# A fused graph network layer on one core: gcn_b moved into the value tiles, one ScalarE pass and a VectorE low half over the mixed blocks

## The chip, the core and the metric

The kernel runs on one core of one Trainium2 chip. The metric is the device time of a launch in microseconds (us), taken as the median of the runs. Below, PE is TensorE, DVE is VectorE, ACT is ScalarE, POOL is GpSimd and SP is SyncE, which here issues the loads and stores.

## The reference

x holds 128 graphs of 64 nodes with 384 features, adj their 0/1 adjacency. gcn_b is a bias of 384 numbers, drawn non-zero here. With an adjacency of only 0 and 1 each edge has the same kind, and the kernel uses that. A path for other adjacencies is branched over on the chip and does not run.

```python
adj = dep_type_matrix != 0
hi_t = einsum('bid,de->bie', h, W1_w[:HID])[:, :, None, :] + (edge term) + W1_b
hj_t = einsum('bjd,de->bje', h, W2_w[:HID])[:, None, :, :] + (edge term) + W2_b
relevance = sum(hi_t * hj_t, axis=-1)
A = softmax(where(adj, relevance, -1e9), axis=2)
h_syn = relu(einsum('bij,bjd->bid', A, h) @ gcn_w + gcn_b)
return layernorm(h + h_syn @ Wo_w + Wo_b)
```

The rows of A sum to one. So a row vector added to every row of h @ gcn_w comes out of A @ (h @ gcn_w) unchanged.

## The kernel before

The 8192 tokens are cut into 16 groups (0 to 15, LAST is 15) of 512 tokens: four "pairs" q of 128 tokens, each two graphs. The three chunks of 128 features are c, d or f in the code (C is 3). For accuracy the large products are done in three passes: an operand is split into a high half (rounded to fp32r) and a low half (the rest), and PE adds high x high, high x low and low x high. These are the three lines L415 to L417 of the helper `three`, and L506, L507 and L512 for the output product.

Each engine runs its own program, written out by hand, group by group in `body(g, par)`, and the engines meet at semaphores only. Groups 2 to 13 run in a loop of two bodies, groups 0, 1, 14 and 15 are written out. In body g the engines do this:

- PE: `mix(g-1)` (L492, the attention weights times the value tiles of the group before), `score_stage(g)` (L437), `value(g+1, q)` for the four pairs (x @ gcn_w into PSUM banks 1 to 4), `out(g-1)` (times Wo), `turn(g)` (L472, transposes the weights), `proj(g+1)`. Body 15 has no value and no projection. Its order is mix(14), score(15), `out` of group 13 pairs 2 and 3, `out` of group 14 pairs 0 and 1, turn(15), `out` of 14 pair 2, mix(15), `out` of 14 pair 3, and then `out_last(15)`.
- ACT: `hidden(g-1)` reads the mixed blocks from PSUM, one block for each chunk f. Blocks 0 and 1 lie in banks 6 and 7, block 2 in banks 4 and 5. For each block it makes two passes of Relu with the bias gcn_b: one writes hs_sb in full precision (L775), one writes the rounded high half hs_hi (L777; in group 14 its home is xt_hi). Then come the exponentials (`weigh`), a rounding of x, `row_terms`, and copies out of PSUM.
- DVE: the masked scores (L914, L918, L920), `value_out` (L819, a copy of the value tile out of PSUM), `low_half(g-1)` (L905, hs_sb minus hs_hi, both in SBUF), the softmax weights (L932, L934), the sum with x (`add_x`, L827), its statistics (L832) and the normalisation (L849).
- POOL: x plus Wo_b (L1098), the low half of x (L1089), the inverse deviation (L1109).

PE waits in three places for what the change touches. `value(g+1, 3)` writes bank 4, where mixed block 2 lies, and waits on `hshi`. `out(g-1)` waits on `hslo` (all low halves). `out` of group 14, pairs 1 and 2, reuses banks in which the output of group 13 lay, and waits until `add_x` of group 13, pair 2 and pair 3, has read them.

At the end, `hidden(15)` on ACT is followed by `normalise_last` for group 13 (L726). That result is stored, and DVE's first `add_x` of group 15 waits for this store (semaphore `stored`), since it writes the same buffer y_sb. After it DVE works through the four pairs of group 15, and POOL, DVE and SP finish each.

## Time and profile before

| what | value |
|---|---|
| median of 3 runs | 389.34 us (389.31 to 390.85) |
| the profiled execution, its own time | 389.31 us |
| its span in the trace | 387.5 us |
| PE busy | 373.5 us (96%) |
| DVE busy | 215.4 us (56%) |
| ACT busy | 170.8 us (44%) |
| POOL busy | 150.4 us (39%) |
| share of PE in the chain that ended last | 90% |

The span is what the trace holds, from the first instruction to the last. The execution's own time is 1.8 us longer. A busy share is an average. A span of 387.5 us with PE busy for 373.5 us leaves 14 us in which PE does nothing, and the question is where in the program they lie.

### The profile page before, as it was taken

To read this page: it belongs to the slowest core of one execution; us is meant where nothing else is said; L and a number is where in the kernel's file an instruction comes from. 1 tells how busy PE (TensorE), PEld (TensorE's weight loads), DVE (VectorE), ACT (ScalarE), POOL (GpSimd) and SP (SyncE) were. 2 spreads that over 40 slices of the span, in tenths; PEclk is the share of its full clock that TensorE was granted. 3 is DMA by queue.
4 is the path that set the end of the run, shared out by engine and by line. 5 is a ranking of instruction groups with operands and counts; after the bars stand their busy time and mean duration, and the time that the engine had idled before them with its cause. 6 is when DMAs were issued, how large, how long until landed. Compare 5 with 4: busy or idle time off the path is not lost.

```text
span 387.5 us, 10043 instructions
## 1 busy us (share of the span) xinstructions
PE 373.5 (96%) x3977; PEld 342.2 (88%) x3977; DVE 215.4 (56%) x528; ACT 170.8 (44%) x389; POOL 150.4 (39%) x133
## 2 busy tenths in 40 slices
PE   8899999999999999999999999999999999999990
PEld 4789898999989899998989899898989989898890
DVE  1635175674637467563646656363765636374954
ACT  1635552616354271625427162633616263444372
POOL 0123454270815326081633608062350807243123
PEclk9999999999999999999999999999999999999997
DMA  7922023508052350706244170614317071531023
GB/s 222 319 99 81 18 82 80 181 10 249 1 181 78 88 169 16 242 0 185 73 106 151 19 238 0 196 61 135 122 24 233 0 216 41 152 109 42 2 83 125
DMA packets 34820, 42.89 MB, mean 111 GB/s; under 512 B 10096, under 2 KB 29040, under 8 KB 34800
## 3 DMA queue, kind: packets, MB, share of 16 engines
q1 hardware_dynamic: 34144, 41.92, 35.9%
q10 hardware_dynamic: 656, 0.70, 0.6%
q8 instruction: 13, 0.21, 0.2%
q14 instruction: 7, 0.06, 0.1%
HBM read 30.03 MB, written 12.58 MB: 110 GB/s over the span
## 4 chain that ended last, share of the span: by engine, by line
PE 90%; DMA 3%; ACT 2%; DVE 2%; POOL 1%; SPq 1%; issue 0%; DVEq 0%
PE banks L415 18%; PE banks L417 17%; PE banks L416 17%; PE banks L506 8%; PE banks L507 8%; PE banks L512 8%; PE banks L492 6%; PE banks L437 6%; DMA gcn_sb<-in_gcn_w_dram 2%; ACT hs_sb L775 1%; PE banks L472 1%; DMA out_dram<-y_sb 1%; POOL rstd L1109 1%; DVE xt_lo L905 0%; ACT xt_hi L777 0%; ACT hs_hi L777 0%
## 5 line engine op out<-in xcount | busy, mean ns | idle before, releaser
L1098 POOL TENSOR_TENSOR x_sb<-x_sb,wob_sb 128x1536 f32<-128x1536 f32 x15 | 52.5, 3503 | 178.0 <-DVE weights L934 178.0
L415 PE MATMUL banks<-gcn_hi,xt_hi 128*128 128x386 f32 x192 | 66.7, 347 | 1.1 <-DVE gcn_lo L877 1.1
L417 PE MATMUL banks<-gcn_hi,xt_lo 128*128 128x386 f32 x192 | 65.0, 339 | 0.0
L416 PE MATMUL banks<-gcn_lo,xt_hi 128*128 128x386 f32 x192 | 65.0, 339 | 0.0
L914 DVE SCALAR_TENSOR_TENSOR rel<-banks,srow,adj_sb 128x64 f32<-128x64 f32 x64 | 13.8, 278 | 86.2 <-PE banks L437 84.8
L506 PE MATMUL banks<-wo_hi,hs_hi 128*128 128x384 f32 x180 | 61.0, 339 | 0.0
L507 PE MATMUL banks<-wo_lo,hs_hi 128*128 128x384 f32 x180 | 61.0, 339 | 0.0
L512 PE MATMUL banks<-wo_hi,hs_lo 128*128 128x384 f32 x180 | 60.6, 339 | 0.0
L701 ACT ACTIVATE gt_sb<-banks,r_sb 128x512 f32<-128x512 f32 x45 | 30.9, 687 | 65.9 <-PE banks L417 65.9
L415 PE MATMUL banks<-xt_hi,m_hi 128*128 128x512 f32 x144 | 57.6, 400 | 0.4 <-DVE hg_sb L819 0.4
L417 PE MATMUL banks<-xt_hi,m_lo 128*128 128x512 f32 x144 | 56.7, 394 | 0.0
L416 PE MATMUL banks<-xt_lo,m_hi 128*128 128x512 f32 x144 | 56.4, 392 | 0.0
L1089 POOL TENSOR_TENSOR xt_lo<-xt_sb,xt_hi 128x1536 fp32r<-128x1536 f32 x15 | 52.6, 3505 | 3.3 <-ACT xt_hi L695 3.3
L827 DVE TENSOR_TENSOR y_sb<-banks,x_sb 128x384 f32<-128x384 f32 x60 | 33.4, 557 | 30.4 <-PE banks L512 30.3
L819 DVE COPY hg_sb<-banks 128x385 f32<-128x385 f32 x64 | 35.6, 556 | 22.2 <-PE banks L417 22.1
L775 ACT ACTIVATE hs_sb<-banks,bias_sb 128x512 f32<-128x512 f32 x48 | 33.4, 695 | 16.3 <-PE banks L492 16.3
L415 PEld LDWEIGHTS banks<-gcn_hi,xt_hi 128*128 128x128 f32 x192 | 36.2, 188 | 2.3 <-issue 1.2
L832 DVE BATCH_NORM_STATS2 stats<-y_sb 128x6 f32<-128x384 f32 x64 | 35.9, 561 | 2.2
L416 PEld LDWEIGHTS banks<-gcn_lo,xt_hi 128*128 128x128 f32 x192 | 36.5, 190 | 0.0
L417 PEld LDWEIGHTS banks<-gcn_hi,xt_lo 128*128 128x128 f32 x192 | 36.3, 189 | 0.0
L789 ACT COPY at_sb<-banks 128x256 f32<-128x256 f32 x16 | 6.0, 374 | 68.0 <-PE banks L472 68.0
L506 PEld LDWEIGHTS banks<-wo_hi,hs_hi 128*128 128x128 f32 x180 | 33.8, 188 | 0.1
(87 smaller groups left out, 580.8 us busy)
## 6 DMA issues: line engine op xcount, KB each, us to landing
xt_sb<-in_x_t_dram SPq DMA_DIRECT2D x15, 768.0 KB, 4.6
x_sb<-in_x_dram SPq DMA_DIRECT2D x15, 768.0 KB, 5.6
out_dram<-y_sb SPq DMA_DIRECT2D x30, 384.0 KB, 5.8
adj_sb<-in_adj_dram SPq DMA_DIRECT2D x32, 64.0 KB, 2.3
xt_sb<-in_x_t_dram SPq DMA_DIRECT2D x2, 384.0 KB, 8.5
xt_sb<-in_x_dram SPq DMA_DIRECT2D x1, 768.0 KB, 6.2
out_dram<-y_sb SPq DMA_DIRECT2D x4, 192.0 KB, 1.9
w1t_sb<-in_w_t_dram ACTq DMA_DIRECT2D x3, 192.0 KB, 6.3
```

Source lines behind the costliest of these rows:

```text
L415: pe.matmul(acc, a_hi, b_hi, start=first, stop=False)
L416: pe.matmul(acc, a_hi, b_lo, start=False, stop=False)
L417: return pe.matmul(acc, a_lo, b_hi, start=False, stop=last)
L506: pe.matmul(acc, hs_home(g)[0][:, c, ts], wo_hi[:, c, :], start=(c == 0), stop=False)
L507: pe.matmul(acc, hs_home(g)[0][:, c, ts], wo_lo[:, c, :], start=False, stop=False)
L512: mm = pe.matmul(out_bank(g, q)[:, 0:HID], hs_home(g)[1][:, c, ts], wo_hi[:, c, :], start=False, stop=(c == C - 1))
L775: act.activation(by_graph(hs_sb[:, f, :]), mixed(f), ACT.Relu, bias=gb_sb[:, f:f + 1]).then_inc(hsr, 1)
L819: dve.tensor_copy(hg_sb[:, slot, q, :], VALUE_BANK[q][:, 0:HID + 1]).then_inc(hg_ready, 1)
L827: dve.tensor_tensor(y_sb[:, slot, q, :], out_bank(g, q)[:, 0:HID], x_home(g, slot)[:, q, :], ALU.add).then_inc(added, 1)
L832: dve.bn_stats(stats[:, q, :], y_sb[:, slot, q, :]).then_inc(statd, 1)
L1089: pool.tensor_tensor(xt_lo[:, slot], xt_sb[:, slot], f32(xt_hi[:, slot]), ALU.subtract).then_inc(xlo, 1)
L1098: pool.tensor_tensor(x_home(g, slot), x_home(g, slot), wob_sb[:].rearrange("p (o n) -> p o n", o=1).to_broadcast([P, PAIRS, HID]), ALU.add ...
```

## The change

gcn_b is no longer ACT's bias. At the start DVE puts it on a diagonal (three tensor_scalar of the identity with gb_sb), PE spreads it over all rows with a matmul of ones into bank 4, and DVE copies it to the tile gb_row. `value_out` becomes a tensor_tensor that adds gb_row to the value tile while it leaves PSUM. ACT then makes one pass for each block, without bias, straight to the high half. The low half is made by DVE from PSUM itself, max(mixed, 0) minus hs_hi, in two instructions for each block, one for each bank. The blocks are taken in the order 0, 2, 1, on ACT, on DVE and in the output product. ACT's pass over block 1 waits until DVE has read block 0, which lies in the same banks. `low_half(g-1)` moves to the head of DVE's body, ahead of the masked scores. PE's wait ahead of `value(g+1, 3)` is on `hslo` now.

```diff
         attn = sb("attn", [P, C, P])
         weights = sb("weights", [P, PAIRS, NODES])
         at_sb = sb("at_sb", [P, MIX])
-        hs_sb = sb("hs_sb", [P, C, GT])
+        gb_diag = sb("gb_diag", [P, HID])
+        gb_row = sb("gb_row", [P, HID + 1])
+        hs_sb = sb("hs_sb", [P, C, P])
         hs_hi = sb("hs_hi", [P, C, GT], F32R)
         hs_lo = sb("hs_lo", [P, C, GT], F32R)
...
+        GB_BANK = bank[4]
+        BLOCKS = 0, 2, 1
...
                 elif q == 3 and not static(g, 1):
-                    pe.wait_ge(hshi, C * (g - 1))
+                    pe.wait_ge(hslo, C * (g - 1))
...
                 acc = out_bank(g, q)[:, 0:HID]
-                pe.matmul(acc, hs_home(g)[0][:, c, ts], wo_hi[:, c, :], start=(c == 0), stop=False)
+                pe.matmul(acc, hs_home(g)[0][:, c, ts], wo_hi[:, c, :], start=(c == BLOCKS[0]), stop=False)
                 pe.matmul(acc, hs_home(g)[0][:, c, ts], wo_lo[:, c, :], start=False, stop=False)
             def out_low(g, q, c):
                 ts = slice(q * P, (q + 1) * P)
                 mm = pe.matmul(out_bank(g, q)[:, 0:HID], hs_home(g)[1][:, c, ts], wo_hi[:, c, :],
-                               start=False, stop=(c == C - 1))
-                if c == C - 1:
+                               start=False, stop=(c == BLOCKS[-1]))
+                if c == BLOCKS[-1]:
                     mm.then_inc(out_mm, 1)
...
+            pe.wait_ge(ones_ready, 1)
+            pe.wait_ge(gb_diag_ready, 1)
+            pe.matmul(GB_BANK[:, 0:HID], ones[:].to_broadcast([P, P]), gb_diag[:],
+                      start=True, stop=True).then_inc(gb_mm, 1)
...
             def out_last(g):
-                for c in range(C):
-                    pe.wait_ge(hshi, C * g + c + 1)
+                for n, c in enumerate(BLOCKS):
+                    pe.wait_ge(hshi, C * g + n + 1)
                     for q in range(2):
-                        if c == 0:
+                        if n == 0:
                             pe.wait_ge(added, PAIRS * (g - 1) + q + 2)
                         out_high(g, q, c)
-                    pe.wait_ge(hslo, C * g + c + 1)
+                    pe.wait_ge(hslo, C * g + n + 1)
                     for q in range(2):
                         out_low(g, q, c)
...
             def hidden(g):
                 act.wait_ge(mix_mm, g + 1)
-                for f in range(C):
-                    act.activation(by_graph(hs_sb[:, f, :]), mixed(f), ACT.Relu,
-                                   bias=gb_sb[:, f:f + 1]).then_inc(hsr, 1)
-                    act.activation(by_graph(hs_home(g)[0][:, f, :]), mixed(f), ACT.Relu,
-                                   bias=gb_sb[:, f:f + 1]).then_inc(hshi, 1)
+                for n, f in enumerate(BLOCKS):
+                    if n == C - 1:
+                        act.wait_ge(hslo, C * g + 1)
+                    act.activation(by_graph(hs_home(g)[0][:, f, :]), mixed(f), ACT.Relu).then_inc(hshi, 1)
...
             def value_out(g, slot, q):
                 dve.wait_ge(value_mm, PAIRS * g + q + 1)
-                dve.tensor_copy(hg_sb[:, slot, q, :], VALUE_BANK[q][:, 0:HID + 1]).then_inc(hg_ready, 1)
+                if static(g, 0) and q == 0:
+                    dve.wait_ge(gb_row_ready, 1)
+                dve.tensor_tensor(hg_sb[:, slot, q, :], VALUE_BANK[q][:, 0:HID + 1], gb_row[:],
+                                  ALU.add).then_inc(hg_ready, 1)
...
             dve.tensor_tensor(c1_sb[:], C_BANK[0][:, 0:C], b1_sb, ALU.add).then_inc(c1_ready, 1)
+            dve.memset(gb_row[:, HID:HID + 1], 0.0)
+            dve.wait_ge(ident_ready, 1)
+            for c in range(C):
+                a = dve.tensor_scalar(gb_diag[:, c * P:(c + 1) * P], ident[:], gb_sb[:, c:c + 1], None, ALU.mult)
+            a.then_inc(gb_diag_ready, 1)
...
+            dve.wait_ge(gb_mm, 1)
+            dve.tensor_copy(gb_row[:, 0:HID], GB_BANK[:, 0:HID]).then_inc(gb_row_ready, 1)
...
-            def low_half(g, chunks):
-
-                for f in chunks:
-                    dve.wait_ge(hsr, C * g + f + 1)
-                    dve.wait_ge(hshi, C * g + f + 1)
-                    dve.tensor_tensor(hs_home(g)[1][:, f, :], hs_sb[:, f, :], f32(hs_home(g)[0][:, f, :]),
-                                      ALU.subtract).then_inc(hslo, 1)
+            def low_half(g, parts):
+
+                for n in parts:
+                    f = BLOCKS[n]
+                    dve.wait_ge(hshi, C * g + n + 1)
+                    for h in range(HALVES):
+                        a = dve.scalar_tensor_tensor(by_graph(hs_home(g)[1][:, f, :])[:, h], mixed(f)[:, h], 0.0,
+                                                     by_graph(f32(hs_home(g)[0][:, f, :]))[:, h], ALU.max,
+                                                     ALU.subtract)
+                    a.then_inc(hslo, 1)
             def body(g, par):
+                if not static(g, 0):
+                    low_half(g - 1, range(C))
                 dve.wait_ge(score_mm, g + 1)
...
                 if static(g, LAST):
                     add_x(g - 2, par, 2)
-                    low_half(g - 1, range(C))
                 elif static(g, 0):
                     value_out(1, 1, 0)
                     value_out(1, 1, 1)
                 else:
                     value_out(g + 1, 1 - par, 0)
-                    low_half(g - 1, range(C))
                     value_out(g + 1, 1 - par, 1)
```

DVE in body 15, before. The rows begin with the masked scores of group 15 (rel), and xt_lo is the home of group 14's low half:

```order
L914 SCALAR_TENSOR_TENSOR rel<-banks,srow,adj_sb 128x64 x4
L918 TENSOR_TENSOR rel<-rel,neg_sb 128x256
L920 TENSOR_REDUCE nmax<-rel 128x4
L827 TENSOR_TENSOR y_sb<-banks,x_sb 128x384
L905 TENSOR_TENSOR xt_lo<-hs_sb,xt_hi 128x512 x3
L932 RECIPROCAL rsum<-psum_row 128x4
L934 TENSOR_TENSOR weights<-prob,rsum 128x256
L832 BN_STATS stats<-y_sb 128x6
L827 TENSOR_TENSOR y_sb<-banks,x_sb 128x384
```

The same place after, from the head of the body:

```order
L925 SCALAR_TENSOR_TENSOR xt_lo<-banks,xt_hi 128x4x64 x6
L938 SCALAR_TENSOR_TENSOR rel<-banks,srow,adj_sb 128x64 x4
L942 TENSOR_TENSOR rel<-rel,neg_sb 128x256
L944 TENSOR_REDUCE nmax<-rel 128x4
L839 TENSOR_TENSOR y_sb<-banks,x_sb 128x384
L954 RECIPROCAL rsum<-psum_row 128x4
L956 TENSOR_TENSOR weights<-prob,rsum 128x256
L844 BN_STATS stats<-y_sb 128x6
L839 TENSOR_TENSOR y_sb<-banks,x_sb 128x384
```

The low half went from behind the first add of group 13 (pair 2) to ahead of the scores, and has six instructions for three.

ACT in body 15, before, with what each waits for: hidden of group 14, the exponentials, the copy of the turned weights, and the first rows of hidden of group 15:

```order
L775 ACTIVATE hs_sb<-banks,bias_sb 128x2x4x64 [waits mix_mm]
L777 ACTIVATE xt_hi<-banks,bias_sb 128x2x4x64
L775 ACTIVATE hs_sb<-banks,bias_sb 128x2x4x64
L777 ACTIVATE xt_hi<-banks,bias_sb 128x2x4x64
L775 ACTIVATE hs_sb<-banks,bias_sb 128x2x4x64
L777 ACTIVATE xt_hi<-banks,bias_sb 128x2x4x64
L767 ACTIVATE prob,psum_row<-rel,nmax 128x64 [waits masked]
L767 ACTIVATE prob,psum_row<-rel,nmax 128x64 x3
L789 COPY at_sb<-banks 128x256 [waits turn_mm]
```

The same place after, up to the normalisation of group 13 (L746):

```order
L787 ACTIVATE xt_hi<-banks 128x2x4x64 [waits mix_mm]
L787 ACTIVATE xt_hi<-banks 128x2x4x64
L787 ACTIVATE xt_hi<-banks 128x2x4x64 [waits hslo]
L777 ACTIVATE prob,psum_row<-rel,nmax 128x64 [waits masked]
L777 ACTIVATE prob,psum_row<-rel,nmax 128x64 x3
L798 COPY at_sb<-banks 128x256 [waits turn_mm]
L787 ACTIVATE hs_hi<-banks 128x2x4x64 [waits mix_mm]
L787 ACTIVATE hs_hi<-banks 128x2x4x64
L787 ACTIVATE hs_hi<-banks 128x2x4x64 [waits hslo]
L746 ACTIVATE y_sb<-y_sb,nmr,rstd 128x384 [waits nmr_ready]
```

Six passes became three, and the third waits for DVE.

DVE at the start of the program, after. The rows run from the vectors c1 and c2 to the first two value tiles:

```order
L875 MEMSET gb_row 128x1
L878 TENSOR_SCALAR gb_diag<-ident,bias_sb 128x128 x3
L882 TENSOR_TENSOR c_sb<-c_sb 128x3
L886 TENSOR_TENSOR xt_lo<-xt_sb,xt_hi 128x3x256
L890 TENSOR_TENSOR gcn_lo<-gcn_sb,gcn_hi 128x384 x3
L894 TENSOR_TENSOR gcn_lo<-banks,gcn_hi 128x2 x3
L897 COPY gb_row<-banks 128x384
L899 TENSOR_TENSOR xt_lo<-xt_sb,xt_hi 128x3x256
L903 TENSOR_TENSOR m_lo<-banks,m_hi 128x384 x3
L830 TENSOR_TENSOR hg_sb<-banks,gb_row 128x385 x2
```

The first two of these rows and the copy to gb_row are new, and everything else stands in the order of before (the last row was two copies). On PE the matmul that spreads gcn_b stands ahead of the small products of line L547 (`r_stage`).

## Rows read from the trace of the kernel before

**Rows 1.** Busy time by engine in a stretch: length, PE, PEld, DVE, ACT, POOL, clock
```profile
200.00:225.00 25.00, 25.00 (x336) 22.91 (x338) 12.90 (x32) 10.73 (x25) 9.34 (x7) 1.00 0.41 120
```

**Rows 2.** Timeline of group 8: start, duration, engine, line, operation
```profile
182.13 0.86 DVE L914 SCALAR_TENSOR_TENSOR rel<-banks,srow,adj_sb 128x64 f32<-128x64 f32 x4 [5.55 <-PE banks L437]
...
186.89 0.34 PE L415 MATMUL banks<-gcn_hi,xt_hi 128*128 128x386 f32 x1
...
194.83 0.38 PE L472 MATMUL banks<-ident,weights 128*128 128x128 f32 x2
```

**Rows 3.** Timeline of the start of the program
```profile
7.08 6.06 PE L539 MATMUL banks<-w2t_sb,w1t_sb 128*128 128x385 f32 x18 [0.44 <-DVE c_sb L861]
...
14.84 0.42 PE L415 MATMUL banks<-gcn_hi,xt_hi 128*128 128x386 f32 x1 [1.14 <-DVE gcn_lo L877]
...
15.74 1.48 DVE L884 TENSOR_TENSOR m_lo<-banks,m_hi 128x384 fp32r<-128x384 f32 x3
...
19.59 0.48 PE L415 MATMUL banks<-xt_hi,m_hi 128*128 128x512 f32 x1
```

**Rows 4.** Groups by line and shape: count, busy us, mean ns of one
```profile
L819 DVE COPY hg_sb<-banks 128x385 f32<-128x385 f32 x64 | 35.6, 556 | 22.2 <-PE banks L417 22.1
L827 DVE TENSOR_TENSOR y_sb<-banks,x_sb 128x384 f32<-128x384 f32 x60 | 33.4, 557 | 30.4 <-PE banks L512 30.3
...
L777 ACT ACTIVATE hs_hi<-banks,bias_sb 128x512 fp32r<-128x512 f32 x45 | 31.4, 698 | 0.0
...
L905 DVE TENSOR_TENSOR hs_lo<-hs_sb,hs_hi 128x512 fp32r<-128x512 f32 x45 | 28.5, 684 | 1.0 <-ACT hs_hi L777 1.0
...
L695 ACT CAST xt_hi<-xt_sb 128x1536 fp32r<-128x1536 f32 x15 | 22.2, 1482 | 20.8 <-DMA xt_sb<-in_x_t_dram 20.8
...
L914 DVE SCALAR_TENSOR_TENSOR rel<-banks,srow,adj_sb 128x64 f32<-128x64 f32 x64 | 13.8, 278 | 86.2 <-PE banks L437 84.8 <-ACT srow L717 1.4
...
L918 DVE TENSOR_TENSOR rel<-rel,neg_sb 128x256 f32<-128x256 f32 x16 | 6.8, 425 | 0.5
...
L789 ACT COPY at_sb<-banks 128x256 f32<-128x256 f32 x16 | 6.0, 374 | 68.0 <-PE banks L472 68.0
```

**Rows 5.** The same view, VectorE alone: 384 columns, from SBUF and from PSUM
```profile
L873 DVE TENSOR_TENSOR gcn_lo<-gcn_sb,gcn_hi 128x384 fp32r<-128x384 f32 x3 | 1.5, 554 | 0.7 <-ACT gcn_hi L735 0.7
L884 DVE TENSOR_TENSOR m_lo<-banks,m_hi 128x384 fp32r<-128x384 f32 x3 | 1.5, 550 | 0.0
```

**Rows 6.** Timeline of body 15, up to the turn and what follows it
```profile
356.84 0.69 ACT L775 ACTIVATE hs_sb<-banks,bias_sb 128x512 f32<-128x512 f32 x1 [0.90 <-PE banks L492]
...
358.37 0.86 DVE L914 SCALAR_TENSOR_TENSOR rel<-banks,srow,adj_sb 128x64 f32<-128x64 f32 x4 [4.25 <-PE banks L437]
...
361.22 1.29 DVE L905 TENSOR_TENSOR xt_lo<-hs_sb,xt_hi 128x512 fp32r<-128x512 f32 x2
...
361.51 0.22 ACT L767 ACTIVATION_READ_ACCUMULATOR prob<-rel,nmax 128x1 f32 x1
362.42 0.17 DVE L932 RECIPROCAL rsum<-psum_row 128x4 f32<-128x4 f32 x1
362.56 0.44 PE L506 MATMUL banks<-wo_hi,xt_hi 128*128 128x384 f32 x1 [0.86 <-DVE xt_lo L905]
...
363.44 0.54 DVE L827 TENSOR_TENSOR y_sb<-banks,x_sb 128x384 f32<-128x384 f32 x1
```

**Rows 7.** Timeline of the tail
```profile
365.93 0.42 PE L506 MATMUL banks<-wo_hi,xt_hi 128*128 128x384 f32 x1
...
369.31 0.42 DVE L949 TENSOR_REDUCE row_max<-adj_max 128x1 f32<-128x256 int32 x1
369.39 0.69 ACT L775 ACTIVATE hs_sb<-banks,bias_sb 128x512 f32<-128x512 f32 x1 [2.80 <-PE banks L492]
...
372.82 2.52 ACT L726 ACTIVATE y_sb<-y_sb,nmr,rstd 128x384 f32<-128x384 f32 x4
...
376.75 0.56 DVE L827 TENSOR_TENSOR y_sb<-banks,xt_sb 128x384 f32<-128x384 f32 x1 [2.83 <-DMA out_dram<-y_sb]
```

More of the change, by code:

```diff
@@ L198, in gnn_layernorm_kernel @@
         c_mm = sem("c_mm")
+        gb_diag_ready = sem("gb_diag_ready")
+        gb_mm = sem("gb_mm")
+        gb_row_ready = sem("gb_row_ready")
         c12_sb_ready = sem("c12_sb_ready")
@@ L230, in gnn_layernorm_kernel @@
         mix_mm = sem("mix_mm")
-        hsr = sem("hsr")
         hshi = sem("hshi")
@@ L306, in hs_home, with mixed, by_graph @@
             return (xt_hi[:, 0], xt_lo[:, 0]) if static(g, LAST - 1) else (hs_hi, hs_lo)
+        def mixed(f):
+            at, b0, b1 = MIX * (f % 2), MIX_BANK[0][f], MIX_BANK[1][f]
+            halves = banks[:, b0:b1 + 1, at:at + MIX]
+            return halves.rearrange("p h (q n) -> p h q n", n=NODES)
+        def by_graph(row):
+            return row.rearrange("p (q h n) -> p h q n", h=2, n=NODES)
         def run(eng, body):
@@ L576, in out @@
                         pe.wait_ge(hg_ready, PAIRS * (g + 2) + 1)
-                    for c in range(C):
+                    for c in BLOCKS:
                         out_high(g, q, c)
@@ L581, in out_last @@
             def out_last(g):
-                for c in range(C):
-                    pe.wait_ge(hshi, C * g + c + 1)
+                for n, c in enumerate(BLOCKS):
+                    pe.wait_ge(hshi, C * g + n + 1)
                     for q in range(2):
-                        if c == 0:
+                        if n == 0:
                             pe.wait_ge(added, PAIRS * (g - 1) + q + 2)
                         out_high(g, q, c)
-                    pe.wait_ge(hslo, C * g + c + 1)
+                    pe.wait_ge(hslo, C * g + n + 1)
                     for q in range(2):
@@ L593, in out_last @@
                 for q in range(2, PAIRS):
-                    for c in range(C):
+                    for c in BLOCKS:
                         out_high(g, q, c)
@@ L751, in _ @@
             row_terms(0, 0)
-            def mixed(f):
-                at, b0, b1 = MIX * (f % 2), MIX_BANK[0][f], MIX_BANK[1][f]
-                halves = banks[:, b0:b1 + 1, at:at + MIX]
-                return halves.rearrange("p h (q n) -> p h q n", n=NODES)
-            def by_graph(row):
-                return row.rearrange("p (q h n) -> p h q n", h=2, n=NODES)
             def weigh(g):
```

## The prediction

> **What bounds the kernel now.** I read the busy times by stretch first. Between 50 and 350 us PE is busy for all 25.00 of every 25 us, at a granted clock of 1.00; one of the twelve stretches is shown, with DVE busy for 12.90 and ACT for 10.73 [rows 1]. So there the time is PE's own work, and taking a pass from ACT buys nothing by itself: the change can gain only at the two ends, and can lose in the middle if it makes PE wait. Second, the timeline of one middle group shows how much room there is. The scores' first DVE instruction starts at 182.13, PE starts value pair 3 at 186.89, and transposes the softmax weights at 194.83 [rows 2]. Third, the start: PE is idle for 1.14 us ahead of its first value tile [rows 3]. Fourth, body 15 and the tail: PE is idle for 0.86 us because DVE's low half of group 14 comes late [rows 6]. And DVE's first add of group 15 waits for a store of group 13, which ACT could normalise only after its six hidden passes [rows 7].
>
> **Prices.** Value tiles: a copy of 385 columns out of PSUM takes 556 ns, an add of a PSUM and an SBUF operand over 384 columns 557 ns [rows 4]. So copy to add costs 0.
>
> ACT's pass: with a bias it takes 698 ns for 512 columns. Without a bias there are 374 ns for 256 columns and 1482 ns for 1536, which makes 0.87 ns a column and 0.60 us for 512 [rows 4]. I take 0.60 us, and a next pass 0.51 us after it. The other end is 0.70 us.
>
> Low half: no row shows this instruction. The nearest are a two-operand DVE instruction with 256 columns, 425 ns, and with 512, 684 ns [rows 4]. Two of 512 follow each other 0.60 us apart (1.29 for two) [rows 6], so 256 columns should follow 0.36 us apart. I take 0.42 us for one and 0.36 + 0.42 = 0.78 us for a block, against 0.68 before. The same form of instruction with 64 columns takes 278 ns [rows 4], where 256 and 512 columns lead to 0.23. The excess of 0.05 may be fixed (it reads a scalar and an integer operand which the low half doesn't), or a second cycle for each column. The second is the upper end: 0.69 us for one, 0.60 apart, 1.29 for a block. The lower end is 0.78 less 0.1, one block at today's price.
>
> The source moves from SBUF to PSUM. The rows have 384 columns from SBUF at 554 ns and from PSUM at 550 [rows 5], no difference. The Trainium skill (VectorE: DVE Perf Modes, section on the TRN2 errata) gives VectorE's fixed part as 58 cycles from SBUF and 120 from PSUM, which would speak against this change: 62 cycles at the page's 0.96 GHz are an estimated 0.065 us for each of the six instructions of a group. By the page the gain below would be about 0.5 us smaller, some 388.4 us. The trace does not agree with it at 384 columns, and I go by the trace.
>
> Hand-over from one engine to another: DVE's low halves end at 361.22 + 1.29 = 362.51, PE starts at 362.56 [rows 6]. I take 0.1 us as an estimate for ACT to DVE and back, where more is to be done than a matmul's start.
>
> **The start.** Added on DVE: a memset and three tensor_scalar of 128 columns while it has nothing due but c12. Added on PE: one fp32 matmul of 384 columns. Nine such (18 passes) take 6.06 us, 0.67 us each. PE has 1.14 us idle just behind it [rows 3], so it ends inside that wait: 0. If it cost more than 1.14 us, what is over would move everything; I keep 0.3 us for that. Added on DVE ahead of the second low half of x: a copy of 384 columns, 0.55 us by its like [rows 4]. It pushes m_lo from 15.74 + 1.48 = 17.22 to about 17.8, and PE wants it at 19.59 [rows 3]. Cost 0, with 1.8 us left.
>
> **The middle, 13 times the same.** Put the mix's end so that ACT starts hidden at 0. In body 15 ACT starts at 356.84 and the scores 1.53 us later, at 358.37 [rows 6]; the middle is alike. After the change, in body 15's clock:
> - ACT block 0: 356.84 to 357.44; block 2 from 357.35 to 357.95.
> - DVE low half 0: 357.54 to 358.32. ACT block 1 waits for it: 358.42 to 359.02.
> - DVE low half 2 until 359.04, low half 1 from 359.12 to 359.90.
> - The scores start at 359.84 in place of 358.37: 1.47 us later.
>
> In the middle's clock the low halves end at 182.13 + 1.53 = 183.66, 3.2 us before value pair 3, which now needs them [rows 2]. Before the change they were ready later than that, and the output product still never waited. The scores' delay passes to the softmax weights. Before, the reciprocal came 4.05 us after the scores in body 15 [rows 6]. Even 4.05 + 1.47 puts it at 187.7, and the turn is at 194.83 [rows 2]. Queued behind the scores on DVE are value tiles 0 and 1, whose banks nobody needs before the end of the output product. POOL starts after the weights, some tenths later, and has over 10 us. SP's adjacency load waits for the scores, but stands ahead of a wait for the output's adds, which is later. So the middle costs and gains 0. ACT's three passes saved, 45 in the middle and more, are free time on an engine that already waits.
>
> **Body 15.** The low half is no longer behind the scores, so PE need not wait for it: it ends at 359.90, and PE comes to it 1.13 us before 362.56, at 361.43. (The idle time is 0.86. PE's matmuls overlap by 0.17 us, and the first after a wait lasts 0.44 for 0.34 [rows 2, 6].) What is late next is the add of group 13, pair 3. Its chain is scores, maximum, exponentials, reciprocal, weights, statistics, add. The exponentials ended at 361.51 + 0.22 = 361.73; they end at 363.20 now, and the reciprocal starts at 363.30 in place of 362.42, 0.88 us later. (Before, it waited for the low halves, now for ACT.) The add goes from 363.44 to 364.32, ends at 364.86, and PE may start output pair 2 of group 14 at 364.96. Its own pace would bring it there at 365.93 - 1.13 = 364.80 [rows 6, 7]. It waits 0.16, so 0.97 us of the 1.13 is kept when mix(15) starts.
>
> **The tail.** hidden(15) on ACT may start at 369.39 - 0.97 = 368.42. But DVE, 0.88 us late since the reciprocal, has caught up only partly. Of that lateness 0.1 goes at its second add of group 14 and 0.38 at its third, where DVE waited before, so row_max starts at 369.71 for 369.31. Low half 0 follows at 370.07 and ends at 370.85, ACT's block 1 starts at 370.95, and group 13's normalisation 0.51 later, at 371.46, in place of 372.82 [rows 7]: 1.36 us sooner. From there to DVE's first add of group 15 it is 376.75 - 372.82 = 3.93 us of ACT and DMA work that doesn't change. DVE's four pairs follow back to back. PE's last output pairs end before DVE needs them, since PE is some tenths ahead as well. So the end moves by 1.36 us.
>
> **Sum.** The profiled execution took 389.31 us, the median is 389.34, and the span is 387.5 (387.5 + 1.8 around it). 389.31 - 1.36 = 387.95; I say 388.0 us. The likeliest case's own range is 387.4 to 388.6.
>
> **Rivals.**
> 1. DVE's low half is slow and the end comes later than before. Mechanism: the ring ACT block 0, DVE low half 0, ACT block 1, low half 1 stands ahead of the scores, and twice in body 15 PE and ACT wait for DVE. With the upper end of 1.29 us a block: the scores start at 361.15 (2.78 late), the reciprocal at 364.61, the add of pair 3 ends at 366.17, and PE is 0.3 us later than before instead of 0.97 earlier. Row_max starts at 371.0, low half 0 ends at 372.7, and the normalisation starts at 373.3, 0.45 late: 389.8 us. It decides from about 0.63 us for one instruction. For it speaks the 278 ns at 64 columns; against it, that two other operands can explain them, and the 557 ns of the PSUM add.
> 2. The gain is taken elsewhere: the store lands when it did or PE's waits in body 15 grow, and the tail keeps only a part. With ACT's pass at 0.70 the same walk gives a gain of 1.1 us; with the store's time of 3.93 stretched by a few tenths, or 0.3 us at the start, 0.5. That is 388.8 us. For it: the chain has five hand-overs that I only estimate.
> 3. More is gained: everything behind the low halves goes at ACT's pace, not DVE's. Then the normalisation starts at 368.42 + 3 x 0.51 = 369.95 and the tail becomes PE's: PE ends 0.97 earlier and DVE's last pair follows it, some 2.0 us in all, 387.3. Against it: row_max on DVE stands in front.
> 4. The middle waits after all: each group would have to lose 0.13 us or more to be seen. It would take low halves 3.2 us later than I put them; 13 x 0.15 = 2 us gives 391.3. Nothing in the rows speaks for it.
>
> **How the numbers follow.** No change can be told within 0.5% of 389.34, from 387.4 to 391.3. Forecast 0.62, rival 1 0.14, rival 2 0.15, rival 3 0.06, rival 4 0.03. The range for 8 in 10 runs from 387.2 to 389.7, the forecast's own range with rival 2 and most of rival 1. Faster by over 0.5% holds rival 3 and the forecast's edge, 0.07; slower holds rival 4 and a little of rival 1, 0.04; no change 0.89.
>
> **What would show it.** Low-half instructions of 128x256 near 0.42 us, ACT's pass near 0.60, the value tile's add near 0.56. Middle stretches still 25.00 busy. The 0.86 us in front of group 14's output gone, and a wait of 0.1 to 0.3 us one product later, for y_sb. Row_max some 0.4 later, the normalisation 1.2 to 1.5 earlier, and the wait for the store smaller. It would be wrong if PE showed a wait in every group, if a low-half instruction took over 0.6 us, or if the matmul for gcn_b moved the first value tile past 14.84.

## The result, and the profile after

| | before | after |
|---|---|---|
| median, on one chip side by side (15 runs each) | 390.51 us | 387.05 us (384.89 to 388.71) |
| ratio of after to before | | 0.990 (0.988 to 0.993) |
| the profiled execution, its own time | 389.31 us | 387.49 us |
| its span | 387.5 us | 385.5 us |
| PE, DVE, ACT busy | 373.5, 215.4, 170.8 us | 373.8, 220.4, 142.6 us |

By the ratio, which goes by the means, the change gains 3.8 us (2.7 to 4.8); the medians are 3.5 apart. The forecast was 1.36. The time lies below the forecast range, if barely.

I cut both spans at the copies of the turned weights (`at_sb`, one for each group), since these follow a fixed place in PE's program. The third column is a kernel that is explained below: the changed one, with hs_hi, hs_lo and what follows them put back to the addresses of before.

| stretch, us | before | after | after, tiles as before |
|---|---|---|---|
| start to the first at_sb copy | 39.17 | 40.48 | 40.21 |
| 14 groups, up to the copy of group 14 | 309.88 | 308.26 | 309.89 |
| to the copy of group 15 (body 15) | 17.16 | 16.00 | 16.03 |
| to the start of DVE's last write of y_sb | 16.60 | 15.56 | 15.54 |
| to the end of the span (the last store) | 4.69 | 5.20 | 4.83 |

Two stretches hold the gain: the groups of the middle, 1.62 us, which I had put at nothing, and body 15 with the tail, 1.16 + 1.04 = 2.20 us, where I had put 1.36. Together they make 3.82 us, as much as the means differ. The start was later by 1.31 us in this one execution, and the last stretch, which ends with a store, longer by 0.5; so these two spans are only 2.0 us apart.

The stretch of the middle after, which answers to [rows 1] (same columns). PE is still busy all the time:

```profile
200.00:225.00 25.00, 25.00 (x314) 22.82 (x315) 13.22 (x35) 9.45 (x22) 9.39 (x7) 1.00 0.43 119
```

So this view can't show the gain: a PE that is never idle can still do a group in less time. The copies of the turned weights show it. First three in a row of before, then three of after (start, duration):

```profile
195.24 0.37 ACT L789 COPY at_sb<-banks 128x256 f32<-128x256 f32 x1 [4.76 <-PE banks L472]
217.67 0.37 ACT L789 COPY at_sb<-banks 128x256 f32<-128x256 f32 x1 [4.76 <-PE banks L472]
240.10 0.37 ACT L789 COPY at_sb<-banks 128x256 f32<-128x256 f32 x1 [4.76 <-PE banks L472]
```

```profile
195.72 0.37 ACT L798 COPY at_sb<-banks 128x256 f32<-128x256 f32 x1 [4.64 <-PE banks L488]
218.02 0.37 ACT L798 COPY at_sb<-banks 128x256 f32<-128x256 f32 x1 [4.65 <-PE banks L488]
240.33 0.37 ACT L798 COPY at_sb<-banks 128x256 f32<-128x256 f32 x1 [4.65 <-PE banks L488]
```

A group took 22.43 us and takes 22.31. Of the groups by line and shape, the output matmuls alone got shorter. Lines of before (a value matmul first), then of after:

```profile
L416 PE MATMUL banks<-gcn_lo,xt_hi 128*128 128x386 f32 x192 | 65.0, 339 | 0.0
L506 PE MATMUL banks<-wo_hi,hs_hi 128*128 128x384 f32 x180 | 61.0, 339 | 0.0
```

```profile
L432 PE MATMUL banks<-gcn_lo,xt_hi 128*128 128x386 f32 x192 | 65.0, 338 | 0.0
...
L522 PE MATMUL banks<-wo_hi,hs_hi 128*128 128x384 f32 x180 | 60.5, 336 | 0.0
...
L528 PE MATMUL banks<-wo_hi,hs_lo 128*128 128x384 f32 x180 | 59.9, 336 | 0.0
```

From the first output matmul of a group to what follows the last it takes 6.24 us in place of 6.35, which is 0.1733 us for each of the 36 in place of 0.1764. These 0.114 us are nearly all of the 0.12; another 0.005 came off the value matmuls. The mean times of the value and projection matmuls stayed within 1 ns.

What answers to [rows 4], with the waits behind the bar:

```profile
L925 DVE SCALAR_TENSOR_TENSOR hs_lo<-banks,hs_hi 128x256 fp32r<-128x256 f32 x90 | 32.7, 418 | 68.0 <-ACT hs_hi L787 67.9
L787 ACT ACTIVATE hs_hi<-banks 128x512 fp32r<-128x512 f32 x45 | 25.3, 596 | 20.9 <-PE banks L508 15.4 <-DVE hs_lo L925 5.5
L830 DVE TENSOR_TENSOR hg_sb<-banks,gb_row 128x385 f32<-128x385 f32 x64 | 34.7, 555 | 23.6 <-PE banks L433 23.6
```

The three prices of the forecast stand: 0.42 us for a low half of 256 columns, 0.60 for ACT's pass, 0.56 for the value tile's add. ACT waits for DVE inside the ring, 5.5 us in all, and PE for neither.

Body 15 after, which answers to [rows 6]:

```profile
356.53 1.08 ACT L787 ACTIVATE xt_hi<-banks 128x512 fp32r<-128x512 f32 x2 [0.90 <-PE banks L508]
357.16 2.18 DVE L925 SCALAR_TENSOR_TENSOR xt_lo<-banks,xt_hi 128x256 fp32r<-128x256 f32 x6 [3.34 <-ACT xt_hi L787]
...
357.95 0.60 ACT L787 ACTIVATE xt_hi<-banks 128x512 fp32r<-128x512 f32 x1 [0.34 <-DVE xt_lo L925]
...
359.25 0.85 DVE L938 SCALAR_TENSOR_TENSOR rel<-banks,srow,adj_sb 128x64 f32<-128x64 f32 x4
...
361.18 0.35 PE L522 MATMUL banks<-wo_hi,xt_hi 128*128 128x384 f32 x1
...
362.52 0.18 DVE L954 RECIPROCAL rsum<-psum_row 128x4 f32<-128x4 f32 x1 [1.04 <-ACT prob L777]
...
364.46 0.42 PE L522 MATMUL banks<-wo_hi,xt_hi 128*128 128x384 f32 x1
```

And the tail, which answers to [rows 7]:

```profile
368.73 0.42 DVE L971 TENSOR_REDUCE row_max<-adj_max 128x1 f32<-128x256 int32 x1
...
369.06 0.74 DVE L925 SCALAR_TENSOR_TENSOR hs_lo<-banks,hs_hi 128x256 fp32r<-128x256 f32 x2
...
369.84 0.60 ACT L787 ACTIVATE hs_hi<-banks 128x512 fp32r<-128x512 f32 x1 [0.83 <-DVE hs_lo L925]
...
370.34 2.49 ACT L746 ACTIVATE y_sb<-y_sb,nmr,rstd 128x384 f32<-128x384 f32 x4
...
374.23 0.56 DVE L839 TENSOR_TENSOR y_sb<-banks,xt_sb 128x384 f32<-128x384 f32 x1 [2.02 <-DMA out_dram<-y_sb]
...
380.30 0.48 DVE L861 TENSOR_SCALAR y_sb<-y_sb,mv,rstd 128x384 f32<-128x384 f32 x1 [0.60 <-POOL rstd L1131]
```

In all these rows the clock stands 0.31 us earlier than before (the mix of group 14 starts at 354.83 for 355.14), so 0.31 is to be added to a time of after when it is held against one of before. PE's wait of 0.86 us for the low half is gone. DVE's first add of group 15 still waits for the store, for 2.02 us where it was 2.83.

### The profile page after: what moved, and what is told of

Its sections match the earlier page's. It is cut to its first block, busy times and chain, and to the rows that moved or that the text cites. A ratio compares the mean times of both kernels' runs of the same rounds, so it can differ in the third digit from the quotient of the medians.

```text
span 385.5 us, 10018 instructions
## 1 busy us (share of the span) xinstructions
PE 373.8 (97%) x3979; PEld 342.0 (89%) x3979; DVE 220.4 (57%) x581; ACT 142.6 (37%) x341; POOL 150.7 (39%) x133
## 4 chain that ended last, share of the span: by engine, by line
PE 92%; DVE 4%; POOL 1%; ACT 1%; DMA 1%; issue 1%; DVEq 0%
PE banks L431 18%; PE banks L433 17%; PE banks L432 17%; PE banks L523 7%; PE banks L528 7%; PE banks L522 7%; PE banks L508 6%; PE banks L453 6%; PE banks L555 2%; PE banks L536 1%; DVE stats L844 1%; PE banks L488 1%; DMA out_dram<-y_sb 1%; DVE y_sb L839 1%; POOL rstd L1131 1%
## 5 line engine op out<-in xcount | busy, mean ns | idle before, releaser
L925 DVE SCALAR_TENSOR_TENSOR hs_lo<-banks,hs_hi 128x256 fp32r<-128x256 f32 x90 | 32.7, 418 | 68.0 <-ACT hs_hi L787 67.9
L830 DVE TENSOR_TENSOR hg_sb<-banks,gb_row 128x385 f32<-128x385 f32 x64 | 34.7, 555 | 23.6 <-PE banks L433 23.6
L777 ACT ACTIVATE prob<-rel,nmax 128x64 f32<-128x64 f32 x64 | 21.5, 337 | 39.5 <-DVE nmax L944 39.5
L523 PEld LDWEIGHTS banks<-wo_lo,hs_hi 128*128 128x128 f32 x180 | 33.8, 188 | 0.0
```

What stands on the lines that cost most here:

```text
L523: pe.matmul(acc, hs_home(g)[0][:, c, ts], wo_lo[:, c, :], start=False, stop=False)
L830: dve.tensor_tensor(hg_sb[:, slot, q, :], VALUE_BANK[q][:, 0:HID + 1], gb_row[:], ALU.add).then_inc(hg_ready, 1)
L925: a = dve.scalar_tensor_tensor(by_graph(hs_home(g)[1][:, f, :])[:, h], mixed(f)[:, h], 0.0, by_graph(f32(hs_home(g)[0][:, f, :]))[:, h], A ...
```

## The experiments

The theories. T1: the middle's 1.6 us come from where hs_hi and hs_lo lie in SBUF, the on-chip memory that all tiles share. They are the stationary tiles of the output product, those that PE loads ahead of each matmul. hs_sb shrank from 6144 to 1536 bytes a partition and gb_diag and gb_row came in, so hs_hi starts at 148800 in place of 150304. Rival: three ACT passes fewer, or other accesses, speed PE up. T2: the tail goes by group 13's normalisation on ACT, its store, and the add that waits for it. T3: the start is hidden. In an edit, pad_a and pad_b are unused columns of four bytes.

**e1, before with hs_hi moved by 32 bytes.**

```diff
+        pad_a = sb("pad_a", [P, 8])
         hs_hi = sb("hs_hi", [P, C, GT], F32R)
         hs_lo = sb("hs_lo", [P, C, GT], F32R)
+        pad_b = sb("pad_b", [P, 8])
         y_sb = sb("y_sb", [P, 2, PAIRS, HID])
```

> The kernel before with 32 bytes of padding ahead of hs_hi and 32 behind hs_lo: these two tiles begin at a multiple of 64 bytes, all others stay within a 64-byte line where they were. Placement theory: output matmuls that read hs_hi and hs_lo start every 0.1735 us instead of 0.177, a group takes 22.31 us instead of 22.43, and the time falls by 1.6 to 1.9 us (ratio 0.995 to 0.996). Rival (the faster groups come from fewer ScalarE passes and less SBUF traffic): nothing changes, ratio 1.000.

Measured: 388.00 us, ratio 0.994 (0.991 to 0.998); a group takes 22.31 us and the output matmul 336 ns; body 15 stays at 17.16. 32 unused bytes bring the whole gain of the middle, and no engine's program is changed.

**e2, after with hs_hi moved by 32 bytes**, the same edit.

> The changed kernel with the same 32 bytes of padding: hs_hi and hs_lo begin 32 bytes past a multiple of 64, as they did before the change. Placement theory: a group takes 22.43 us again, and 1.6 to 1.9 us of the gain are lost (ratio to before about 0.994 to 0.995). Rival (fewer passes): groups stay at 22.31 us, ratio 0.990.

Measured: 385.74 us, 0.990 (0.986 to 0.993); 22.33 us a group. So "32 past a multiple of 64 is slow" fell.

**e5, after with hs_lo and what follows moved, not hs_hi** (pad_a behind hs_hi).

> The changed kernel with padding between hs_hi and hs_lo only: hs_hi begins at a multiple of 64 bytes, hs_lo 32 past one. If the place of the stationary tile itself counts, only the output matmul that reads hs_lo (one in three) is slower, and a group takes 22.35 us, between 22.31 and 22.43. If it is a matter of hs_hi alone, 22.31.

Measured: 386.7 us in a single run, 22.30 us a group. hs_lo's place within 64 bytes doesn't matter to the group here. But the single passes shifted against each other: the output matmuls have means of 335, 334 and (with hs_lo) 338 ns for 336, 336 and 336, and the projection's of 404, 388 and 393 for 399, 392 and 394, though no tile of the projection had moved. e2, where hs_lo lies at the same address, has the projection at 403, 389 and 392. So the mean of one pass is weak evidence for a place; the group's period is what I go by.

**e6, after with the rows of gcn_hi and gcn_lo lengthened to 1600 bytes.**

```diff
-        gcn_hi = sb("gcn_hi", [P, C, HW], F32R)
+        gcn_hi = sb("gcn_hi", [P, C, HID + 16], F32R)[:, :, 0:HW]
```

> The changed kernel with the rows of gcn_hi and gcn_lo, the streamed operand of the value matmuls, padded from 1544 to 1600 bytes, so that each of their six rows begins at a multiple of 64. If the place of a streamed operand counts too, the value matmuls go from 0.176 to 0.174 us, a group gets 0.05 to 0.1 us shorter and the time 0.8 to 1.5 us. If only the stationary tile's place counts: no change against the changed kernel, ratio to before 0.990.

Measured: 386.71 us, 0.992 (0.989 to 0.995); 22.39 us a group, slower by 0.08. What changed is the projection. Its streamed tiles xt_hi and xt_lo were moved by the edit, by 320 bytes, and m_hi and m_lo stayed. Its 27 matmuls of a group take 6.45 us for 6.37, with means of 404, 395 and 394 ns for 399, 392 and 394. So places have a price in other products too. The 404 ns alone would not show it, since e5 has them as well, at no cost to the group. The value matmuls gained nothing by the longer rows (6.46 us a group for 6.45).

**e9, e10, e11: other pads**, 96 bytes (after), 96 bytes (before), 160 bytes (after).

> The kernel after with 96 bytes (per partition) put ahead of hs_hi: it starts at 148896, which is 32 bytes past a multiple of 128, as in the kernel before (150304); hs_lo and y_sb move by 96 and 128. Theory A, the output product is slower when its stationary tile starts 32 past a multiple of 128: a group of the middle takes 22.43 us as before, and the output matmul has a mean of 339 ns. Rival B, the position within 128 bytes doesn't matter: 22.31 to 22.33 us and 336 ns.

> The kernel before with 96 bytes put ahead of hs_hi: it starts at 150400, a multiple of 128, where the pad of 32 bytes had put it 64 past one. Theory A: 22.31 us for a group of the middle. Rival B, the slow place of the kernel before is one single address and any move away from it helps: 22.31 us too, so this run can't tell A from B; it can only make both fall, with 22.43 us. Theory C, the group's time goes by something else that the pad of 32 bytes changed by chance: anything from 22.31 to 22.43.

> The kernel after with 160 bytes put ahead of hs_hi: it starts at 148960, 96 bytes past a multiple of 128, the class that the pad of 32 bytes gave (22.33 us). Theory A: 22.33 us again. Rival B: 22.31 to 22.33. With 22.39 or more the period goes by whole addresses, not by their place within 128 bytes.

Measured: 22.33, 22.32 and 22.31 us a group (385.8, 387.8 and 385.6 us, single runs). Theory A, 32 past a multiple of 128, fell with e9.

**e13, after with every tile from hs_hi on at its address of before** (pad_a of 376 columns, 1504 bytes).

> The kernel after with 1504 unused bytes per partition ahead of hs_hi. Then hs_hi (150304), hs_lo (156448), y_sb (162592) and every tile behind them start exactly where they do in the kernel before; the program is otherwise the kernel after. Theory P, the place of the tiles alone gave the middle's 1.6 us: 22.42 or 22.43 us for a group of the middle, a mean of 339 ns for the output matmul, and a time about 1.6 us above that of the kernel after, ratio some 0.995. Rival Q, the gain in the middle comes from the change itself (three ACT passes less, or reads of PSUM in place of SBUF) and the pads of the earlier runs did something else: 22.31 us, ratio 0.990.

Measured: 388.54 us, 0.993 (0.989 to 0.998). Its output matmul, and its line for the low half's product:

```profile
L523 PE MATMUL banks<-wo_hi,hs_hi 128*128 128x384 f32 x180 | 61.0, 339 | 0.0
...
L529 PE MATMUL banks<-wo_hi,hs_lo 128*128 128x384 f32 x180 | 60.5, 339 | 0.0
```

The copies of the turned weights come 22.43 us apart again:

```profile
196.29 0.37 ACT L799 COPY at_sb<-banks 128x256 f32<-128x256 f32 x1 [4.76 <-PE banks L489]
218.72 0.37 ACT L799 COPY at_sb<-banks 128x256 f32<-128x256 f32 x1 [4.76 <-PE banks L489]
```

With ACT's passes, VectorE's reads of PSUM and every other instruction as in the kernel after, the addresses alone bring the 1.6 us back. The rival Q fell by this period; the ratio's interval would hold both 0.995 and 0.990. Body 15 and the stretch behind it keep the times of after (16.03 and 15.54 us), so their gain is the change's own.

**e14, before with y_sb alone moved; e15, before with all three moved by 128 bytes; e16, after with all three moved by 96.**

> The kernel before with 32 bytes put ahead of y_sb alone: hs_hi and hs_lo stay at 150304 and 156448, y_sb and what follows it move from 162592 to 162624. Theory P1, the place of the output product's own operand sets its pace: 22.43 us for a group, 339 ns. Rival P2, the tile that the other engines write meanwhile (y_sb) does: 22.31 us, 336 ns.

> The kernel before with 128 bytes ahead of hs_hi: hs_hi 150432, hs_lo 156576, y_sb 162720, all three still 32 bytes past a multiple of 128. Theory P3, it is the place within 128 bytes of all three together (the earlier pads broke it for one of them each time): 22.43 us. Rival P4, whole addresses decide: any other value, 22.31 the likeliest.

> The kernel after with 96 bytes ahead of hs_hi and none ahead of y_sb: hs_hi 148896, hs_lo 155040, y_sb 161184, all three 32 bytes past a multiple of 128 as in the kernel before, but 1408 bytes lower. Theory P3: 22.43 us. Rival P4: 22.31 to 22.33.

Measured: 22.43, 22.33 and 22.33 us a group. e14 shows that moving y_sb and what follows takes no part, so it is the place of the product's own operands, hs_hi and hs_lo. Neither of the two was moved alone from the slow place, so which of them counts is open. e15 and e16 let P3 fall. All places of hs_hi together:

| hs_hi at | kernels | us a group | output matmul, ns |
|---|---|---|---|
| 150304 | before, e3, e13, e14 | 22.43 | 339 |
| 150336, 150400, 150432 | e1, e10, e15 | 22.31, 22.32, 22.33 | 334 to 337 |
| 148800 | after, e4, e5, e7, e8, e12, e17, e18 | 22.30 to 22.31 | 334 to 338 |
| 148832, 148896, 148960 | e2, e9 and e16, e11 | 22.33, 22.33, 22.31 | 336 to 337 |
| 149120 | e6 | 22.39 (projection) | 336 |

One place of nine is slow, and no rule on the place within 64 or 128 bytes that I tried picks it out. That the place decides is shown; what is special about it stays open.

**e3 and e4, an earlier normalisation**, in before and in after: group 13's pairs 2 and 3 are normalised ahead of `hidden(15)`.

```diff
+                    normalise_last(LAST - 2, 1, 1, (2, 3))
                     hidden(g)
...
             run(act, body)
-            normalise_last(LAST - 2, 1, 1, (2, 3))
```

> The kernel before, with ScalarE's last normalisation of group 13 put ahead of the hidden passes of group 15, where ScalarE sits idle for 2.8 us. Tail theory (the end is set by hidden passes, then this normalisation, then its store, then the first add of group 15): the wait of 2.8 us for the store goes, the first add starts when PE has its product (about 374.4 instead of 376.75 in the trace), 2.2 to 2.4 us gained, ratio 0.994. Rival (the tail is set by the output product on PE): 0 to 0.3 us.

> The changed kernel with the same move. Tail theory: the first add of group 15 starts at about 372.7 instead of 374.2, 1.5 us gained on the changed kernel, ratio to before about 0.986. Rival: nothing, 0.990.

Measured: 387.97 us, 0.993 (0.990 to 0.997), and 385.03 us, 0.986 (0.981 to 0.991). The first add of group 15 in e3, then in e4:

```profile
373.50 0.56 DVE L827 TENSOR_TENSOR y_sb<-banks,xt_sb 128x384 f32<-128x384 f32 x1 [0.47 <-PE banks L512]
```

```profile
371.27 0.56 DVE L839 TENSOR_TENSOR y_sb<-banks,xt_sb 128x384 f32<-128x384 f32 x1 [0.52 <-PE banks L528]
```

The wait for the store is gone in both and PE is what comes last. T2 holds: it was ACT's hidden passes ahead of the normalisation that set the tail. Counted from the copy of group 15, the last write of y_sb comes 2.34 us sooner in e3 and 1.51 in e4, as expected. e4 has the lowest median of all kernels, but its interval holds the 0.990 of after too; the trace is what shows the 1.5 us.

**e7, after with the low half at its old place on DVE**, behind the first value tile or add.

```diff
-                if not static(g, 0):
-                    low_half(g - 1, range(C))
                 dve.wait_ge(score_mm, g + 1)
...
                     add_x(g - 2, par, 2)
+                    low_half(g - 1, range(C))
```

> The changed kernel with VectorE's low half back where it stood, behind the masked scores and the first value tile. The exponentials on ScalarE then stand behind the third hidden pass, which waits for the first low half. My walk: in the middle the low halves end just about when value pair 3 wants them, at most 0.1 us of wait in a group; in body 15 PE waits for them by 1 to 2 us again. So 1 to 3 us slower than the changed kernel, ratio to before 0.993 to 0.998. Rival (the order does not matter, the saved passes do): 0.990.

Measured: 387.35 us, 0.994 (0.992 to 0.996). A group of the middle takes 22.31 us as ever, so the order on DVE is worth nothing there. Body 15 takes 17.44 us in place of 16.00, since PE waits for the low half again:

```profile
363.81 0.44 PE L522 MATMUL banks<-wo_hi,xt_hi 128*128 128x384 f32 x1 [1.17 <-DVE xt_lo L925]
```

All of body 15's gain of 1.16 us hangs on the move to the head; with the new passes at the old place it would be a loss of 0.28. The tail gives 0.50 of it back, so body 15 and tail together are 0.94 us longer than in after, where I had expected 1 to 3. The order 0, 2, 1 of the blocks was not run alone.

**e8 and e12, the matmul for gcn_b put between the chunks of the weights' product**, alone and with the edit of e4.

```diff
             for c in range(C):
+                if c == 1:
+                    pe.wait_ge(ones_ready, 1)
+                    pe.wait_ge(gb_diag_ready, 1)
+                    pe.matmul(GB_BANK[:, 0:HID], ones[:].to_broadcast([P, P]), gb_diag[:],
+                              start=True, stop=True).then_inc(gb_mm, 1)
```

> The changed kernel with the matmul that spreads gcn_b moved ahead, between the first and second third of the product W1 x W2, where PE waits for the weights' loads. In the changed kernel's trace it stood on PE's path at the start, 0.65 us. Theory: where the loads come late it is hidden, 0 to 0.65 us gained, mean some 0.4. Rival: it was hidden in most runs anyway, 0. The spread of the runs makes this hard to tell by time; the trace shows the place.

> The kernel after with two edits that each have been run alone: the normalisation of group 13, pairs 2 and 3, issued ahead of hidden of group 15 on ACT, and the matmul for gcn_b put between the chunks of the weights' product at the start. Theory: the first add of group 15 waits for PE, not for the store, and starts about 3 us sooner than in the kernel after (about 371.3 on the same start), and the first value tile doesn't wait for the matmul. The early normalisation alone gave a ratio of 0.986 to the kernel before, the matmul in the gap nothing beyond the kernel after; so 0.985, some 384.5 to 385.2 us. Rival: the two share the gain and the ratio stays at 0.990.

Measured: 385.71 us, 0.991 (0.987 to 0.994), and 385.46 us, 0.987 (0.984 to 0.990). Neither is better than the same kernel without the edit, within the intervals, and e12 misses the 384.5 to 385.2 that I expected. The traces say why. In e8, then in e12:

```profile
6.20 2.18 PE L560 MATMUL banks<-w2t_sb,w1t_sb 128*128 128x385 f32 x6 [0.43 <-DVE c_sb L874]
8.22 0.81 PE L554 MATMUL banks<-gb_diag,ones 128*128 128x384 f32 x2
8.86 4.05 PE L560 MATMUL banks<-w2t_sb,w1t_sb 128*128 128x385 f32 x12
```

```profile
7.33 4.19 PE L560 MATMUL banks<-w2t_sb,w1t_sb 128*128 128x385 f32 x6 [0.43 <-DVE c_sb L874]
11.31 1.49 PE L554 MATMUL banks<-gb_diag,ones 128*128 128x384 f32 x2
12.59 4.40 PE L560 MATMUL banks<-w2t_sb,w1t_sb 128*128 128x385 f32 x12
```

PE waited for no load there. The matmul takes 0.64 us of its time in e8 and 1.28 in e12, where the first six matmuls of the product are slow too (4.19 us for 2.18).

**e17 and e18, after without the work for gcn_b at the start, and after once more.** In e17 gcn_b isn't added at all.

```diff
+            dve.memset(gb_row[:], 0.0).then_inc(gb_row_ready, 1)
...
-            pe.matmul(GB_BANK[:, 0:HID], ones[:].to_broadcast([P, P]), gb_diag[:],
-                      start=True, stop=True).then_inc(gb_mm, 1)
...
-                a = dve.tensor_scalar(gb_diag[:, c * P:(c + 1) * P], ident[:], gb_sb[:, c:c + 1], None, ALU.mult)
...
-            dve.tensor_copy(gb_row[:, 0:HID], GB_BANK[:, 0:HID]).then_inc(gb_row_ready, 1)
```

> The kernel after without its work for gcn_b at the start: no diagonal, no matmul of ones, no copy; gb_row is set to zero by one memset, so gcn_b isn't added at all. The value tiles still add the row. Theory, the work at the start is hidden (as forecast): the same time as the kernel after within 0.5 us (0.990, about 1.0 against it), and a first value tile that waits for gcn_lo where the weights' product takes 6.06 us. Rival: the start costs about 1.3 us, as the profiled runs could suggest (the first copy of turned weights comes at 39.8 us on average in nine kernels with this work, and at 38.4 in six without): ratio 0.987, and this kernel's first such copy near 38.4.

> The kernel after, unchanged, on the same chip and with the same runs of before as the kernel without the work for gcn_b. Ratio 0.990 under both; the difference to the other run tells what the start costs. In its profile the first matmuls of the weights' product last either 0.49 us (then the first value tile starts near 14.8 us) or 0.98 us (then 1 to 3 us later): what decides is not in the kernel, by every theory.

Measured: 385.77 us, 0.992 (0.989 to 0.995), and 385.84 us, 0.992 (0.989 to 0.995). The means of the two are 0.02 us apart, with an interval of some 1.4 us to either side. So no cost of the start's work shows, but the times alone don't exclude the rival's 1.3 us. The gain of the change repeats. The first copy of turned weights comes at 39.58 us in e17, not near the rival's 38.4. Both profiled executions have the long weights' product, and there the work does stand on PE's path. In e18:

```profile
7.33 7.80 PE L555 MATMUL banks<-w2t_sb,w1t_sb 128*128 128x385 f32 x18 [0.43 <-DVE c_sb L873]
14.97 0.81 PE L568 MATMUL banks<-gb_diag,ones 128*128 128x384 f32 x2
15.62 0.72 PE L563 MATMUL banks<-c_sb,w2t_sb 128*128 128x1 f32 x6
16.20 0.42 PE L431 MATMUL banks<-gcn_hi,xt_hi 128*128 128x386 f32 x1
```

The matmul for gcn_b holds PE for 0.65 us (14.97 to 15.62) and PE doesn't wait ahead of the value tile. From the product's end to the value tile it is 1.07 us in e18 and 0.42 in e17 without it. So it costs up to 0.65 us where the product takes 7.5 or more. Where it takes 6.06 us the work is hidden: in the traces of e2, e4, e6 and e16 PE still waits for gcn_lo ahead of the first value tile, for 0.28 to 1.39 us.

## Why the prediction was wrong, point by point

- **"So the middle costs and gains 0."** This is the step that failed. The waits were read rightly: PE waits for nothing there, before or after. But I priced only the instructions that the change names. The 486 output matmuls between the first copy and that of group 14 kept their lines and shapes and still came 3.2 ns closer to each other (486 x 0.0032 = 1.54 us of the 1.62 measured, with 0.07 more in the value product), since a smaller tile ahead of theirs had moved them. The 0.1735 and 0.177 us in the expectation of e1 were rough readings of the same spacing. e1 and e13 show it from both sides. The rows of before could not tell that 150304 was a slow place. They held one hint: the output matmuls, with 384 columns, took as long as the value matmuls with 386 (339 ns), where after they are shorter.
- **The prices.** Low half 0.42 us, ACT's pass 0.60, the add 0.555: right. The two low halves of a block came 0.33 us apart for 0.36. Rival 1 fell with them. With 256 columns the form with one operand in PSUM took 418 ns, beside 425 ns of another two-operand form out of SBUF [rows 4]. The Trainium skill (VectorE: DVE Perf Modes, section on the TRN2 errata) gives VectorE a fixed part of 120 cycles from PSUM and 58 from SBUF. The traces do not agree with that difference, neither here nor in one and the same form at 384 columns (550 and 554 ns) [rows 5].
- **Hand-overs of 0.1 us.** They took 0.03 to 0.06: ACT's block 1 starts at 357.95, 0.05 after the low half's end (357.16 + 0.74). The scores came 1.19 us later for 1.47 (counted from the mix of group 14), and the reciprocal 0.41 for 0.88.
- **Body 15, PE.** The wait of 0.86 went. The wait of 0.16 that I expected one product later did not come, because the reciprocal and the add were earlier than I put them: pair 2 starts 1.16 us sooner for 0.97.
- **The tail, "1.36 us sooner": the term that was mis-sized.** It measured 2.17 at the normalisation (370.34 + 0.31 for 372.82). The sum had row_max 0.40 later than before; it came 0.27 earlier (368.73 + 0.31 for 369.31). DVE was 0.41 late at the reciprocal and not 0.88. It also made up more on the way than the 0.48 us of idle time that I took off: its adds of group 14 had waited for PE before, whose output now came 1.16 us sooner. From the statistics to the second add it is 0.47 us for 0.66, and from the aggregation to the third 0.17 for 0.62, which gives back 0.64. From row_max on the chain went as forecast: low half, hand-over, block 1, 0.50 later the normalisation, and 3.89 us (for 3.93) to the add. The third add of group 14 before, then after:

```profile
367.80 0.56 DVE L827 TENSOR_TENSOR y_sb<-banks,x_sb 128x384 f32<-128x384 f32 x1 [0.38 <-PE banks L512]
```

```profile
367.25 0.53 DVE L839 TENSOR_TENSOR y_sb<-banks,x_sb 128x384 f32<-128x384 f32 x1
```

- **Rival 3** gave 2.0 us for body 15 and the tail, close to the 2.2 measured, but by a way that isn't there: ACT does wait for DVE (0.83 us ahead of block 1), and the tail isn't PE's until the normalisation goes first (e4).
- **The start: hidden.** Right within what the times resolve, and in the traces with a product of 6.06 us; up to 0.65 us of it shows where the product is long.
- **The chances.** 0.89 for no change followed from a sum with one term missing. All bounds were on operations that the change names.

## What to carry to other kernels

A change that adds, removes or resizes a tile in SBUF also moves every tile behind it, and on a kernel bound by PE that alone was worth 0.4% here, three quarters of what the change itself brought. Put the tiles back to their old addresses with a pad before an edit is credited with a gain, and try a pad of 32 bytes as an edit of its own. Where a chain of two engines takes the place of one, its cost is read at the next point where both meet a third: a delay of DVE was gone there because PE, for which DVE had waited, was earlier.

## What the runs showed of the hardware that was not expected

- The pace of an output matmul (fp32r, 128x384) depends on where hs_hi and hs_lo, its stationary tiles, lie: 339 ns against 336 ns (0.1764 against 0.1733 us from start to start), over 540 matmuls, in four kernels with hs_hi at 150304 and in none of the others.
- The first matmuls of the weights' product are slow in some executions, with the same instructions ahead of them on PE. In the profile of after they start 0.64 us apart until 10.67 us, then 0.32 apart; one lasts 0.85 us and then 0.49, and the very first, behind a wait, 0.98 for the 0.56 of before. The same line in the profile of before and of after, with shortest, median and longest of one:

```profile
L539 PE MATMUL banks<-w2t_sb,w1t_sb x18: 484/487/562, 7.1 to 12.7; 128*128 128x385 f32 x18
```

```profile
L555 PE MATMUL banks<-w2t_sb,w1t_sb x18: 484/487/981, 7.3 to 14.6; 128*128 128x385 f32 x18
```

Seven of the twenty profiled kernels had it (7 of 14 with the change, none of 6 without), and their product took 7.5 to 9.1 us for 6.06, or 9.7 in e12 with the matmul for gcn_b inside. The spacing is twice as long, as between TensorE's levels of 1.2 and 2.4 GHz, and the clock entries kept in the traces fit. The first entry, of 1.00, begins at 10.76 us of the span in after, while the first short matmul runs. It begins at 10.2 to 13.4 us in the seven and at 4.4 to 6.2 in the other thirteen (6.23 in before). The views print 1.00 for the time ahead of it as well, but no entry stands there. PE had been at work since 1.3 us in all twenty.

e17 has it without the work for gcn_b. Between before and after the product begins 0.25 us later, lasts 1.69 longer, and the way from its last matmul to the first value tile is 0.63 shorter, which makes the 1.31 us of the start. It will also be a good part of the spread between runs of one kernel, which is not shown. Whether something in the changed kernel favours it is open: if nothing does, all seven would fall on these fourteen once in 23 times.
